# A recurrence of 2048 dependent steps: the last factor formed in another order, and ScalarE's order of small operations changed

## The reference, cut to what matters

```
def step(h, inp):
    x_t, dt_t, B_t, C_t, xr_t = inp
    h_carrier = h.mean(axis=1)
    T = jnp.cos((c_phase(xr_t) - c_phase(h_carrier)) / 2.0) ** 2
    alpha = jnp.exp(dt_t[..., None] * A_neg)
    expo = 1.0 + (1.0 - alpha) * KAPPA * (1.0 - T[:, None, :])
    mag, ph = (c_mag(h), c_phase(h))
    cmag = jnp.minimum(jnp.exp(expo * jnp.log(mag + 1e-08)), 10.0)
    h = from_polar(cmag, ph)
    Bx = B_t[:, None, :, :] * (dt_t * x_t)[:, :, None, None]
    h = h + Bx
    h = from_polar(jnp.tanh(c_mag(h)), c_phase(h))
    y_t = jnp.einsum('bnc,bdnc->bd', C_t, h)
    return (h, y_t)
```

## Time and profile before

| what | value |
|---|---|
| median of 3 runs | 12826.88 us |
| the profiled execution's own time | 12837.53 us |
| its span | 12835.7 us |
| from the first to the last instruction of the recurrence, about | 266 to 9556 us |
| DVE busy in the span | 9759.4 us |
| ACT busy in the span | 8162.1 us |
| TensorE clock granted in the recurrence | 0.50 of full speed |

### The profile page before, as it was taken

The page is one execution under the profiler, slowest core; times in us unless marked ns, Lnnn a source line. Parts: engine busy times, 40 slices in busy tenths (PEclk is TensorE's granted clock), DMA queues, the critical chain, the costliest instruction groups (busy, mean ns, idle before and its releaser), DMA issues. The chain is left out here.

```text
span 12835.7 us, 220415 instructions
## 1 busy us (share of the span) xinstructions
PE 5755.6 (45%) x52526; PEld 4270.2 (33%) x52542; DVE 9759.4 (76%) x56587; ACT 8162.1 (64%) x42451; POOL 94.5 (1%) x164
## 2 busy tenths in 40 slices
PE   5222222222222222222222222222237978888998
PEld 5222222222222222222222222222234546653335
DVE  5777777777777777777777777777774948868875
ACT  6666666666666666666666666666663732264665
POOL 0000000000000000000000000000000100000000
PEclk8555555555555555555555555555558979998999
DMA  1000100001000000001000010000100000011100
GB/s 56 14 14 14 21 14 14 14 14 21 14 14 14 18 17 15 14 14 20 16 14 14 14 21 14 14 14 14 21 10 12 1 23 6 1 37 48 31 24 21
DMA packets 339459, 227.53 MB, mean 18 GB/s; under 512 B 27662, under 2 KB 324183, under 8 KB 337884
## 3 DMA queue, kind: packets, MB, share of 16 engines
q1 hardware_dynamic: 338140, 213.30, 7.8%
HBM read 187.41 MB, written 25.43 MB: 17 GB/s over the span
## 5 line engine op out<-in xcount | busy, mean ns | idle before, releaser
L534 PE MATMUL scan_p_car<-scan_hs,scan_mean_mat 32*32 32x2 f32 x16392 | 579.6, 198 | 6583.9 <-DVE scan_hb L661 6571.2
L534 PEld LDWEIGHTS scan_p_car<-scan_hs,scan_mean_mat 32*32 32x32 f32 x16392 | 403.7, 136 | 6762.8 <-DVE scan_hb L661 6749.9
L579 ACT ACTIVATE scan_act_ps<-scan_act_ps 128x64 f32<-128x64 f32 (+1 forms) x8193 | 1635.1, 200 | 65.5
L579 ACT ACTIVATE scan_act_ps<-scan_state_ps 128x64 f32<-128x64 f32 x2048 | 426.0, 208 | 1879.4 <-DVE scan_state_ps L658 1879.4
L561 PE MATMUL scan_p_y<-scan_c_masked,scan_hb 128*64 128x4 f32 x16384 | 1234.2, 253 | 0.0
L539 PE MATMUL scan_p_car<-scan_eps_row,ones 1*128 1x3 f32 x4102 | 1197.9, 360 | 39.1 <-DMA scan_a_log<-L_attn_a_A_log 38.9
L661 DVE SCALAR_TENSOR_TENSOR scan_uw<-scan_w,scan_rsq 128x64 f32<-128x64 f32 x2048 | 461.4, 225 | 853.4 <-ACT scan_rsq L579 853.4
L561 PEld LDWEIGHTS scan_p_y<-scan_c_masked,scan_hb 128*64 128x64 f32 x16384 | 1055.4, 216 | 34.2
L539 PEld LDWEIGHTS scan_p_car<-scan_eps_row,ones 1*128 1x128 f32 x4102 | 1020.4, 308 | 72.0 <-DMA scan_a_log<-L_attn_a_A_log 39.3
L579 ACT ACTIVATE scan_power_ps<-scan_state_ps,scan_s 128x64 f32<-128x64 f32 x2049 | 591.1, 288 | 673.3 <-DVE scan_s L684 673.3
L658 DVE TENSOR_TENSOR scan_c<-scan_V,scan_power_ps 128x64 f32<-128x64 f32 x4096 | 723.7, 218 | 366.8 <-ACT scan_power_ps L579 304.7
(11 more groups left out here) (450 smaller groups left out, 17412.8 us busy)
## 6 DMA issues: line engine op xcount, KB each, us to landing
scan_step_in<-scan_scratch SPq DMA_DIRECT2D x520, 256.0 KB, 6.2
qk_scratch<-qkv_parts SPq DMA_DIRECT2D x32, 384.0 KB, 2.5
attn_qT<-qk_scratch SPq DMA_DIRECT2D x192, 64.0 KB, 2.2
attn_kT<-qk_scratch SPq DMA_DIRECT2D x192, 64.0 KB, 2.2
scan_scratch<-prep_dts SPq DMA_DIRECT2D x32, 256.0 KB, 2.1
x<-L_attn_a_x SPq DMA_DIRECT2D x1, 4096.0 KB
out<-x SPq DMA_DIRECT2D x1, 4096.0 KB
filter_in_taps<-c_kT SPq DMA_DIRECT2D x1, 2048.0 KB
```

Of the source, the lines that this page charges most:

```text
L534: last = nc.tensor.matmul(p_car[slot][rows, 0:2], mean_mat[rows, :], hs[rows, :], start=False, stop=True)
L579: nc.scalar.activation(dst, src, func, **kw).then_inc(counts[par]["act"], 1)
```

## The change

On DVE `F` is gone. In its place, and earlier in the order, stands `Vm`, the state times (magnitude + 1e-8), 2 x 64 wide on 128 partitions, which waits for `mag` and `hp`. `V` becomes `Vm` times the reciprocal norm `ru`, and waits for `ru` and `Vm`. On ACT the square of the carrier (`nsq`) comes right behind `mag`, then `lm`, `lnn`, `lnh`, `rs`, `ru`, where before it was `lnh`, `nsq`, `ru`, `lnn`, `lm`, `rs`. No operation of ACT is added or taken away.

```diff
--- before.py
+++ after.py
@@ -404,8 +404,8 @@
 
 
 
-DVE_STEP = ["c0", "c1", "w0", "w1", "sq0", "sq1", "na", "r2", "n2", "bx0", "bx1", "uw0", "uw1", "h0", "h1", "nh", "hp", "dot", "F", "dl", "s", "V"]
-ACT_STEP = ["al", "l", "M", "ln2", "E", "rsq", "L1", "R", "th2", "l2", "mag", "lnh", "nsq", "ru", "lnn", "lm", "rs", "cm"]
+DVE_STEP = ["c0", "c1", "w0", "w1", "sq0", "sq1", "na", "r2", "n2", "bx0", "bx1", "uw0", "uw1", "h0", "h1", "nh", "hp", "Vm", "dot", "dl", "s", "V"]
+ACT_STEP = ["al", "l", "M", "ln2", "E", "rsq", "L1", "R", "th2", "l2", "mag", "nsq", "lm", "lnn", "lnh", "rs", "ru", "cm"]
 PE_STEP = ["carrier", "y"]
 STEPS = {"dve": (DVE_STEP, "h0"), "act": (ACT_STEP, "l2"), "pe": (PE_STEP, "carrier")}
 
@@ -446,8 +446,8 @@
         a_neg, a_log, a_pos = ph.sb("a_neg", [P, 1]), ph.sb("a_log", [P, 1]), ph.sb("a_pos", [P, 1])
         alpha = ph.sb("alpha", [P, 2, J])
         hb = ph.sb("hb", [P, 2, 3, J])
-        c, w, sq, uw, bx, V = (ph.sb(n, [P, 2, J]) for n in ("c", "w", "sq", "uw", "bx", "V"))
-        na, rsq, R, th2, mag, ru, F = (ph.sb(n, [P, J]) for n in ("na", "rsq", "R", "th2", "mag", "ru", "F"))
+        c, w, sq, uw, bx, Vm, V = (ph.sb(n, [P, 2, J]) for n in ("c", "w", "sq", "uw", "bx", "Vm", "V"))
+        na, rsq, R, th2, mag, ru = (ph.sb(n, [P, J]) for n in ("na", "rsq", "R", "th2", "mag", "ru"))
         act_ps, state_ps, norm_ps, power_ps = (ph.ps(n, [P, 512]) for n in ("act_ps", "state_ps", "norm_ps", "power_ps"))
         lr, E2, ln2, M, L1, l2, lnh = (act_ps[:, q * J:(q + 1) * J] for q in range(7))
         r2, dl = (state_ps[:, q * J:(q + 1) * J] for q in range(2))
@@ -584,18 +584,18 @@
                     op(par, l2[:, :], th2[:, :], ACT.Ln, bias=EPS_MAG)
                     after(act, "act", "l2", par, k)
                     op(par, mag[:, :], l2[:, :], ACT.Exp, scale=0.5)
+                    after(act, "pe", "carrier", par, k)
+                    op(par, squares[:, :], p_car[slot][:, 0:3], ACT.Square, accum_out=nsq[:, :])
+                    after(act, "act", "mag", par, k)
+                    op(par, lm[:, :], mag[:, :], ACT.Ln, bias=EPS_MAG)
+                    after(act, "act", "nsq", par, k)
+                    op(par, lnn[:, :], nsq[:, :], ACT.Ln)
                     after(act, "dve", "nh", par, k)
                     op(par, lnh[:, :], nh[:, :], ACT.Ln)
-                    after(act, "pe", "carrier", par, k)
-                    op(par, squares[:, :], p_car[slot][:, 0:3], ACT.Square, accum_out=nsq[:, :])
+                    after(act, "act", "lnn", par, k)
+                    op(par, rs[:, :], lnn[:, :], ACT.Exp, scale=-0.5)
                     after(act, "act", "lnh", par, k)
                     op(par, ru[:, :], lnh[:, :], ACT.Exp, scale=-0.5)
-                    after(act, "act", "nsq", par, k)
-                    op(par, lnn[:, :], nsq[:, :], ACT.Ln)
-                    after(act, "act", "mag", par, k)
-                    op(par, lm[:, :], mag[:, :], ACT.Ln, bias=EPS_MAG)
-                    after(act, "act", "lnn", par, k)
-                    op(par, rs[:, :], lnn[:, :], ACT.Exp, scale=-0.5)
                     after(act, "dve", "s", par, k)
                     op(par, cm[:, :], dl[:, :], ACT.Exp, scale=s_[:, 0:1])
 
@@ -673,17 +673,19 @@
                     after(dve, "act", "th2", par, k)
                     stt(sem, nh[:, :], hb[:, slot, 2, :], 2 * EPS_PHASE, th2[:, :], ALU.mult, ALU.add)
                     nc.vector.tensor_scalar(hb[:, slot, 0, :], hb[:, slot, 2, :], EPS_PHASE, None, ALU.add).then_inc(sem, 1)
+                    after(dve, "act", "mag", par, k)
+                    after(dve, "dve", "hp", par, k)
+                    stt(sem, Vm[:, :, :], mag[:, :].unsqueeze(1).to_broadcast([P, 2, J]), EPS_MAG, hb[:, slot, 0:2, :], ALU.add, ALU.mult)
                     after(dve, "act", "nsq", par, k)
                     stt(sem, products[:, :], p_car[slot][:, 0:2], 1.0, tab[:, nxt, k_nxt, 2:4], ALU.mult, ALU.mult, accum_out=dot[:, :])
-                    after(dve, "act", "ru", par, k)
-                    stt(sem, F[:, :], mag[:, :], EPS_MAG, ru[:, :], ALU.add, ALU.mult)
                     after(dve, "act", "lm", par, k)
                     stt(sem, dl[:, :], alpha[:, (k + 1) % 2, :], 1.0, lm[:, :], ALU.subtract, ALU.mult)
                     after(dve, "act", "rs", par, k)
                     after(dve, "dve", "dot", par, k)
                     nc.vector.tensor_scalar(s_[:, :], rs[:, :], dot[:, 0:1], -0.25, ALU.mult, ALU.add).then_inc(sem, 1)
-                    after(dve, "dve", "F", par, k)
-                    tt(sem, V[:, :, :], hb[:, slot, 0:2, :], F[:, :].unsqueeze(1).to_broadcast([P, 2, J]), ALU.mult)
+                    after(dve, "act", "ru", par, k)
+                    after(dve, "dve", "Vm", par, k)
+                    tt(sem, V[:, :, :], Vm[:, :, :], ru[:, :].unsqueeze(1).to_broadcast([P, 2, J]), ALU.mult)
 
                 def output(par, t0, k):
```

## The result

The changed kernel takes 12729.15 us (median of 4 runs, 12726.58 to 12732.81) against 12826.23 us before: a ratio of 0.9925, 95% interval 0.9908 to 0.9943. The profiled execution took 12732.81 us, 104.7 less than the one before. A second set of runs of the same kernel beside the last experiment gave 0.9926 (0.9913 to 0.9940). So it is faster, by 97 us where 147 were forecast: inside the stated range, outside the forecast's own.

The account below looks back on a forecast made before the run. Bound: a ring of short dependent ACT and DVE instructions, run 2048 times. dl's 0.05 and the square's 0.02 give 0.075 at s, taken as 0.073 a step: 147 us, to 12680; own range 12646 to 12707, whole range 12635 to 12755.

Parts of the forecast that it names:

- What sets `s`: DVE: s is held by dl plus DVE's pitch of 0.14, dl by a late lm; removing this gains 0.05 a step.
- The square's 0.02: ACT: with only mag ahead of it, nsq starts at 4.70 instead of 4.72, making s 0.02 sooner.
- The lower bound of 0: ACT: least gain allowed for moving the square, nsq staying at 4.72; the other bound was 0.07.
- Rival B: ACT: PE sets nsq, which stays at 4.72; only dl's 0.05 is gained, 106 us, giving 12720; chance 0.08.
- `lnn` and `rs`: ACT: lnn starts at 4.93, 0.12 behind lm; rs at 5.14, 0.15 behind lnh, ending at 5.30.
- Small terms behind it: ACT and DVE: rs lasts from 5.14 to 5.30; cm and c follow s at the present 0.24 and 0.32.
- `V` as the next to arrive: DVE: V ends at 5.78 and, with a second wait of 0.10, would release c at 5.88, 0.015 before cm.
- rival A: DVE: V arrives last and releases c at 5.92 to 5.94; gain 0.03 to 0.05, 12725 to 12766; chance 0.13.
- `Vm` costs nothing in its slot: DVE: Vm holds the queue 0.20, to 4.91, while products can't start before 4.93 anyway.
- Rival D: DVE: slower, Vm plugs the queue ahead of products; nothing lost to a hold of 0.355, whole gain at 0.43; chance 0.04.
- Rival C: DVE: rs already sets s, with a hand-off of 0.09; gain only 0.02, 41 us, giving 12786; chance 0.04.

Follow-up runs that it names:

- Experiment 1: Changed kernel with ScalarE's old order put back (lnh, nsq, ru, lnn, lm, rs), Vm and late V kept: 12823.08 us, ratio 1.0007 to the kernel before.
- experiment 7: Changed kernel without lm, dl using l2 in SBUF, lnh ahead of nsq, ru ahead of rs, dl ahead of Vm: 12779.74 us, ratio 0.9973.
- experiment 2: Changed kernel with lnh put ahead of the square nsq again: 12721.05 us, ratio 0.9928 to the kernel before.
- experiment 3: Changed kernel with lnh ahead of nsq and ru ahead of rs: 12720.86 us, ratio 0.9927 to the kernel before.
- experiment 4: Changed kernel with the two waits of c swapped, V first, then cm: 12855.78 us, ratio 1.0035 to the kernel before.
- experiment 6: Changed kernel's ScalarE order, but F kept behind s on VectorE and Vm left out: 13213.96 us, ratio 1.0312 to the kernel before.
- experiment 5: Changed kernel with a second, useless Vm into a spare tile straight behind the first: 12810.54 us, ratio 0.9997 to the kernel before.
- experiment 8: Changed kernel without lm, dl using l2 in PSUM, lnh ahead of nsq, ru ahead of rs: 12701.21 us, ratio 0.9909 to the kernel before.

## Why the prediction was right in direction and half too high in size

- **What sets `s`**: right. That `dl`, held by a late `lm`, and DVE's pitch set `s` was read from starts alone, since no wait showed it. Experiment 1 puts it back and the gain is gone. This term was sized at 0.05, and the whole gain measured at `c` is 0.05.
- **The square's 0.02**: this is the step that failed. "I take 0.02, by the row in which ACT waits as it will" took the start of `nsq` for the result. The start did move (0.52 to 0.50), but the operation took 0.16 for 0.13 and the read ended at 0.72, no sooner. The step of the earlier trace rows shows it, with the row behind it:

```profile
1132.05 0.15 ACT L579 ACTIVATION_READ_ACCUMULATOR scan_act_ps<-scan_p_car 128x1 f32 x1
```

  This read ends at 1132.20, 0.29 behind PE's end at 1131.91. In the earlier trace rows it is 0.28 (4.63 to 4.91), though there `nsq` starts 0.09 behind PE's end and here 0.07. The prediction itself held that PE was the last arrival, and then nothing that frees ScalarE sooner can gain. Its sign for that was wrong: `nsq` starts 0.14 behind `lnh` in experiment 7 too, with the carrier long there, so its start was set by ScalarE's queue and its end by PE. The lower bound of 0 was the true value. Rival B had nearly the right time (12720 as written; 0.05 times 2048 is 102 and not 106, which makes it 12724), but asked for `nsq` to stay put, so its mark in the profile would have missed it.
- **`lnn` and `rs`**: two errors that cancelled, by luck. `lnn` was set 0.12 behind `lm`; it is 0.15 (4010.08 to 4010.23), as `rs` stands behind `lm` in the earlier trace rows. With the late read that makes `lnn` 0.04 late, and it ends 0.03 later than forecast, its row being shorter (0.15 for 0.17). But `rs` was set 0.15 behind `lnh`, and no such hold is there: it starts 0.13 behind `lnh`, 0.03 behind the end of `lnn` (4010.38 to 4010.41). So `rs` came at 0.95 for the forecast 0.94, and 0.01 sooner than before, though the reason given for it had failed. What gave it that is `lm` out of its way (experiments 1 and 2).
- **Small terms behind it**: `rs` starts 0.01 later than forecast, takes 0.17 for 0.16, and `s` to `cm` is 0.25 for 0.24. Together 0.03 by the printed rows, which is what lies between `c` at 1.695 and at 1.72, and so the whole of what the forecast has too much: 0.025 times 2048 is 51 us.
- **`V` as the next to arrive**: right, and closer than forecast. It starts at 1.32 (forecast 1.30) and takes 0.29 (0.28), so it would release `c` 0.01 before `cm` does. Experiments 2 and 3 show that `cm` rules, experiment 4 confirms the 0.10 of the second wait, experiment 6 what rival A costs. Had the second wait cost 0.12, A would have been the case.
- **`Vm` costs nothing in its slot**: right, as was its hold of 0.20: in experiment 5 two such operations together hold the queue for 0.41 us (4011.59 to 4012.00), 0.21 and 0.20. Rival D, in which nothing is lost up to a hold of 0.355, fell with that.
- **Rival C** (`rs` sets `s` already) fell: `s` now starts 0.03 behind the end of `rs`.

## What to carry to other kernels

In a ring of small dependent operations compare every start with the ends of all its inputs and with the instruction ahead of it on its own engine: an operation that is issued late behind a busy neighbour can be missing from the list of waits. Before the change that list has `s` waiting behind `dl` for 16 steps alone, 3.3 us in all, though in the step of the earlier trace rows `dl` holds it by 0.05. Price a step that is moved by when its result is there, from rows in which it ran in the same situation, not by its start. And where an operation has two waits, put the one that arrives last first: for `c` that was 0.03 us from its end against 0.10 (experiment 4).

## What the runs showed of the hardware

- A wait that stands second ahead of `c` on VectorE cost 0.10 us from the end of what it waits for (`cm` in experiment 4, `V` in experiment 6), a first one 0.03 (`cm` in experiment 2, 4011.20 to 4011.23). Swapping two lines cost 141 us over 2048 steps (experiment 4).
- The row of the square is 0.16 us long in the change, 0.13 in experiment 2 and 0.10 in experiment 7, where PE's row for the carrier ended 0.17 ahead of it (0.07 and 0.10 in the other two). The accumulator read follows 0.07, 0.04 and 0.02 behind its start. In the first two the read ends 0.72 behind `l2` alike. That the row begins while the square still waits for the carrier is inferred from these lengths; no row shows it.
- `mag` holds ScalarE for 0.12 us ahead of `lnh` where it reads PSUM (experiment 8), and for 0.16 where it reads SBUF (experiment 7); its own row grows from 0.22 to 0.26. `lm`, which reads SBUF, holds it for 0.15 (ahead of `lnn` in the change, ahead of `rs` in the earlier trace rows). The source isn't all: `lnh` reads PSUM and holds it for 0.14 ahead of the square, in experiment 7 too.
- A scalar-tensor-tensor of 128 columns on two fp32 inputs in SBUF holds VectorE for 0.20 to 0.21 us, though its row is 0.29 long (experiment 5).
